# The order of the odd spreads around the sampling in a deformable convolution

## The reference

```python
om = conv3x3(x, w_off) + b_off
off_y, off_x, mask = om[:, :9], om[:, 9:18], sigmoid(om[:, 18:])
py = off_y + row + ky;  px = off_x + column + kx
sampled = bilinear(x, py, px) * mask
out = einsum('bckhw,ock->bohw', sampled, w) + b
```

## Time and profile before

| what | value |
|---|---|
| median of three runs | 2334.54 us (2331.11 to 2341.95) |
| profiled execution, span | 2334.2 us |
| PE matmul busy over the span | 1539.5 us, 66% |
| DVE busy | 1558.4 us, 67% |
| ACT busy | 1449.8 us, 62% |
| weight loader busy | 1050.0 us, 45% |
| first to last even copy of the main loop | 701.80 to 2102.34 us |

### The profile page before, as it was taken

One profiled execution on the slowest core, in us unless ns is written; L12 is line 12 of the kernel. 1 busy time (PEld: TensorE's weight loads), 2 busy tenths in 40 slices (PEclk: granted clock), 3 DMA queues, 4 the chain that ended last, 5 costly groups with the idle time before them and its releaser, 6 DMA issues. The chain is left out here.

```text
span 2334.2 us, 61913 instructions
## 1 busy us (share of the span) xinstructions
PE 1539.5 (66%) x24206; PEld 1050.0 (45%) x24207; DVE 1558.4 (67%) x1718; ACT 1449.8 (62%) x2219; POOL 606.7 (26%) x1168
## 2 busy tenths in 40 slices
PE   4755980000008888888898898898888898891620
PEld 4632330000006666666665566666665666660310
DVE  5342006656717888888888788888887888883105
ACT  2221224344218898888898898898887898890102
POOL 2000000000033444444443444444444444430000
PEclk9688995555558999999999999999999999996555
DMA  2177874667675666666666666566666656640008
GB/s 116 32 190 184 233 218 159 215 227 275 235 214 126 151 147 157 149 149 155 150 148 152 148 149 157 149 150 157 149 146 150 152 147 157 149 100 22 3 0 338
DMA packets 288861, 362.19 MB, mean 155 GB/s; under 512 B 61853, under 2 KB 260820, under 8 KB 285014
## 3 DMA queue, kind: packets, MB, share of 16 engines
q1 hardware_dynamic: 209552, 226.57, 37.6%
q0 software_dynamic: 36864, 59.94, 11.2%
q10 hardware_dynamic: 42182, 72.05, 9.0%
HBM read 253.94 MB, written 104.39 MB: 154 GB/s over the span
## 5 line engine op out<-in xcount | busy, mean ns | idle before, releaser
L758 POOL DMA_DIRECT2D rows<-scratch_parts x1152 | 583.1, 514 | 821.1 <-PE ps_even_y L790 798.8
L799 PE MATMUL ps_odd_y<-rows,sel 32*128 32x504 f32 (+2 forms) x928 | 459.8, 496 | 502.5 <-DMA rows<-scratch_parts 345.2
L939 DVE TENSOR_TENSOR G<-odd_y,ps_odd_v 128x1008 f32<-128x1008 f32 (+2 forms) x464 | 542.0, 1168 | 182.5 <-PE ps_odd_v L816 182.4
L816 PE MATMUL ps_odd_v<-tent_x,stage 32*128 32x171 f32 (+2 forms) x5568 | 591.1, 318 | 0.0
L947 DVE TENSOR_TENSOR G<-even_v,ps_even_y 128x1008 f32<-128x1008 f32 (+2 forms) x464 | 539.3, 1162 | 23.6 <-ACT even_v L895 21.7
L816 PE MATMUL ps_even_v<-tent_x,stage 32*128 32x171 f32 (+3 forms) x5568 | 541.9, 324 | 8.5 <-DMA stage<-scratch_xt 8.3
L889 ACT COPY odd_y<-ps_odd_y 128x504 f32<-128x504 f32 (+2 forms) x928 | 526.4, 567 | 21.4 <-PE ps_odd_y L799 17.1
L895 ACT COPY even_v<-ps_even_v 128x1008 f32<-128x1008 f32 (+2 forms) x464 | 450.2, 970 | 134.6 <-PE ps_odd_v L816 126.5
L834 PE MATMUL ps_r<-G,conv_w 128*32 128x224 f32 (+1 forms) x8832 | 483.3, 346 | 13.2 <-ACT res L900 13.1
L799 PEld LDWEIGHTS ps_odd_y<-rows,sel 32*128 32x128 f32 x928 | 173.0, 186 | 689.8 <-issue 350.5
L816 PEld LDWEIGHTS ps_odd_v<-tent_x,stage 32*128 32x128 f32 x5568 | 477.8, 190 | 0.0
(11 more groups left out here) (134 smaller groups left out, 913.5 us busy)
## 6 DMA issues: line engine op xcount, KB each, us to landing
place<-scratch_px SPq DMA_DIRECT2D x960, 105.0 KB, 3.4
scratch_parts<-parts ACTq DMA_DIRECT2D x18, 3136.0 KB, 16.7
rows<-scratch_parts POOLq DMA_DIRECT2D x960, 52.5 KB, 3.4
x<-scratch_xh SPq DMA_DIRECT2D x48, 406.0 KB, 5.9
place<-scratch_px SPq DMA_DIRECT2D x192, 84.0 KB, 2.7
scratch_om<-om ACTq DMA_DIRECT2D x64, 196.0 KB, 7.1
rows<-scratch_parts POOLq DMA_DIRECT2D x192, 42.0 KB, 2.6
scratch_conv<-res SPq DMA_DIRECT2D x448, 14.0 KB, 1.8
```

Source lines behind the costliest of these rows:

```text
L758: pool.dma_start(bass.AP(tensor=rows[b][:].tensor, offset=32 * g * pitch + here, ap=[[2 * pitch, Y_KINDS], [GROUP * W, 3], [1, count * W]] ...
L799: nc.tensor.matmul(ps_odd_y[:, lo:hi], sel[32 * g:32 * g + 32, :], taps(rows, 32 * g, 32, p, lo, hi), start=True, stop=True).then_inc(odd_ ...
L816: m = nc.tensor.matmul(sub(ps_v[g // 2], 0, 128, i * 512 + lo + first, dims), stage[32 * g:32 * g + 32, j * IMAGE + v * C:j * IMAGE + (v + ...
L939: nc.vector.tensor_tensor(two(G, ROW, v, slot(v)), two(odd_y[p % 3], ROW, v), two(ps_v[1], 512, v), ALU.mult).then_inc(odd_weighted, 1)
```

## The change

PE's queue in a step becomes: the first two column groups of sample(p), spread_odd(p + 1, 0), the third group, spread_even(p), spread_odd(p + 1, 1), reduce. The wait for fresh rows moves with the first odd spread. ACT copies the first odd image of step p + 1 in its step p - 1, so its queue becomes keep_even(p), keep_odd(p + 1, 1), distance(p + 2), keep_odd(p + 2, 0), result; one such copy comes before the loop. The wait of keep_odd for a free buffer is one step less strict, n - 2 for n - 1.

```diff
-                def sample(it, p):
+                def sample(it, p, to):
...
                     for j, (x0, x_lo, x_hi) in enumerate(COLUMNS):
+                        if j == 2 and to:
+                            rows_ready(*to)
+                            spread_odd(*to, 0)
...
-                        sample(it, p)
+                        sample(it, p, to)
                         spread_even(it, p)
                         if to:
-                            rows_ready(*to)
-                            spread_odd(*to, 0)
+                            spread_odd(*to, 1)
                         if at := block_of(it, p):
...
                             reduce(*at)
-                        if to:
-                            spread_odd(*to, 1)
...
                     if i == 0:
-                        wait(act, odd_weighted, n - 1)
+                        wait(act, odd_weighted, n - 2)
...
                 keep_odd(0, 0, 1)
+                keep_odd(0, 1, 0)
...
                         keep_even(it, p)
                         if to := ahead(it, p + 1, last):
-                            keep_odd(*to, 0)
+                            keep_odd(*to, 1)
                         if to := ahead(it, p + 2, last):
                             distance(*to)
-                        if to := ahead(it, p + 1, last):
-                            keep_odd(*to, 1)
+                            keep_odd(*to, 0)
```

## The result

The changed kernel takes **2452.1 us** (2441.8 to 2455.3), the kernel before 2334.0: a ratio of 1.050, 95% interval 1.048 to 1.053. It is 118 us slower, where 131 us were forecast (2465, range 2350 to 2560). The profiled execution has a span of 2449.9 us.

A forecast was written before the change was run, and what follows sets the result against it. A ring of waits through ACT's copies and the sampling, 2.94 us a step, was taken as the bound; 3.17 us steps plus longer reductions and stalls gave 95.86 for 87.72 us a pair, +130 us: 2465, range 2350 to 2560.

The forecast's parts named there:

- The bound: Kernel before: no engine full; waits through even copy, first odd copy, second odd spread and sampling set the 2.94 us step.
- the new ring: Changed step: part of sampling, first odd spread, its copy, second spread, reduction, next sampling; 3.17 us, chance 0.66.
- the one link that the trace did not have: From the first sampling matmul to the spread in the middle of the sampling: 0.68 us, bounds 0.53 to 0.83.
- The drain: Switching between 32-row and 128-row tiling empties PE: idle 0.24 us before and 0.36 us after each reduction.
- the 0.36: Idle time of the weight loader after a reduction's loads, before the next 32-row work: 0.36 us.
- The longer reductions: Reductions of 20 to 36 loads, hidden before, now count in full: 4.18 us a pair of images.
- 0.3 to 0.6 more in steps with 20 to 36 loads: Expected in the profile after: even copies 3.17 us apart in plain steps, this much further apart with longer reductions.
- The stalls: Mostly ACT's result waiting for the last store, and slower steps after: 3.5 us a pair before, 1.2 kept.
- The clock: Rival: PE slows after long waits; about 2555 us if one step in ten is hit; chance 0.15.
- The price of a slow step: A step of the changed kernel at the lower clock takes 5.16 us.
- the overlapping reduction: Rival: PE enters and leaves the reduction without idling, or the first odd copy is early; 2256 us, chance 0.12.
- the next ring: Sampling, DVE's odd product, next sampling: sets the step at 2.72 us if the main chain of waits falls below that.

The follow-up runs named there:

- The extra copies: Changed kernel plus one more ACT copy of 224 columns into a spare tile: ahead of the first odd copy 2571.1 us, ahead of the second 2442.7 us.
- two tiles: Kernel before with two tiles for the result in place of one, so ACT waits for the store before last: 2295.1 us, 0.984.
- the filled step: Changed kernel with eight more matmuls, result overwritten, in step 4 of a pair, the one step without a reduction: 2404.6 us, 1.031.
- the reversed test: Kernel before with only the second odd spread moved directly behind the first, ahead of the reduction: 3074.8 us, 1.318.

## Why the prediction was right

**The bound and the new ring** were as forecast, link by link: 0.59 for 0.68 to the middle spread, 0.55 for 0.49 + 0.04, 0.63 for 0.58 + 0.06, 0.42, and 0.89 for 0.90. The 3.09 us step is 0.08 under the 3.17, all of it the one link that the trace did not have: the spread is issued ahead of the first matmul of the third group, 1810.30 against 1810.42, not at its time. That makes 0.08 x 28 x 16 = 36 us too much in the sum. The extra copies show that the first odd copy is on the ring and the second beside it.

**The drain.** 0.24 and 0.36 us stood idle as forecast around each plain reduction, and the 0.90 came out. But the 0.36 is not a fixed price behind the last load, as the forecast took it. Behind 20 loads the loader idles 0.08 us, behind 36 loads 0.17:

```profile
1229.04 1.11 PEld L837 LDWEIGHTS ps_r<-G,conv_w 128*32 128x32 f32 x36 [0.24 <-issue]
1230.32 0.19 PEld L819 LDWEIGHTS ps_even_v<-tent_x,stage 32*128 32x128 f32 x2 [0.17 <-issue]
...
1229.04 1.35 PE L837 MATMUL ps_r<-G,conv_w 128*32 128x112 f32 x36
```

What is fixed is the distance to the matmuls. In 423 of the 443 reductions of the changed kernel that a sampling follows, the sampling's first load starts 0.07 us before the end that the profile gives for the reduction's last matmul (it models these ends): 1230.32 against 1230.39 here, 1809.71 against 1809.78 in the plain step. None starts earlier; of the 20 that start later 16 stand at the seam of two pairs. The reduction starts at the same distance from the spread ahead of it, 1811.90 against 1811.97. The rule of the Trainium skill (TensorEngine Tiling (Array Packing), Key Properties), that a change of tiling mode drains TensorE, agrees with these rows. No run was without them, so how large the part is that comes from the mode alone is not shown.

**The longer reductions**: the term of 4.18 us a pair was half wrong. A plain last quarter costs what was said: steps of 3.82 and 2.77 around it, 0.41 more than two of 3.09. But split strips cost nothing. The mis-sized step of the sum is that it added the idle 0.36 to a longer loading time. A reduction with 20 loads in the changed kernel, and the sampling behind it:

```profile
1222.85 0.81 PEld L837 LDWEIGHTS ps_r<-G,conv_w 128*32 128x32 f32 x20 [0.24 <-issue]
```

```profile
1223.74 0.41 PE L819 MATMUL ps_even_v<-tent_x,stage 32*128 32x171 f32 x2
```

It loads for 0.81 in place of 0.54 and the sampling still starts 0.89 later; steps 14 and 15 take 3.09 and 3.10. In the last quarter it is the same: the sampling comes 1.27 us behind the start of 24 loads and 1.28 behind that of 36. The columns streamed, the same number split or not, set the length, and the loader's end does not. So the sign "0.3 to 0.6 more in steps with 20 to 36 loads" came true at the last quarters only. The trace of the kernel before had it already, on PE: the matmuls of the 20 loads of the earlier trace rows lasted 0.97 us, those of 16 loads 0.96. This is 1.5 us a pair, 24 us too much.

**The stalls** were forecast to leave 1.2 of 3.5 us a pair; no wait for a store is left, since four steps now take 12.8 us for 11.8. 19 us too much. That also means that the order itself costs more than 118 us: the kernel before carries 38 us of stalls which a slower loop hides. And the 3.5 were not all stalls: two tiles took off 2.4, and in the trace of that run 0.9 a pair is left in slow steps at a lower clock.

**The clock**, a rival with 0.15, came true in part beside the forecast's case and not in place of it: some 48 us by the filled step. The sign that the forecast had set for it, a granted clock below 0.95 in the middle of the loop, was met in one stretch (0.93). The price of a slow step was right (5.16 against 4.97 to 5.06); where it would fall was not said, and that step 4 lacks its reduction stood in the text of the kernel. The holes of the earlier trace rows cut in three, 0.64, 0.24 and 0.36, leave the clock at 1.00 in plain steps, as argued.

So the sum was 36 + 24 + 19 us too high and the clock 48 too low, which leaves 31 too high; the forecast was 13 above. Of the other 18 us some 5 are three slow steps in the last pair and some 4 the slow start of the first pair; the last 9 are not assigned. The mechanism was right, but the close total is partly luck: errors of 79 and 48 us cancelled.

**The rivals**: the overlapping reduction is out, by the 0.36 of each step and by the 4.08 us step of the reversed test. That the mechanism decides at a given amount off the ring is right, but not the price at which the next ring takes over: I had it at 2.72, and with the spread behind the first third it is 2.86.

## What to carry to other kernels

An instruction that waits for another engine belongs behind the work that can fill its wait, not ahead of it: ask for each wait in an in-order queue what stands behind it, and add that to the ring. When a handover is moved earlier, check how the distance to its partner is covered; here 0.3 us, one column group, decided between 5% slower and 0.4% faster. And look at steps that lack a part of the work: they may lower the clock for the ones behind, and filling them with useless matmuls was worth 13 and 48 us in two kernels.

## What the runs showed of the hardware

- A step with PE busy for 1.77 of 3.00 us was followed, in 12 of the 15 pairs behind the first, by a fall of the granted clock to 0.50 for one to three steps (5.0 us for 3.09). With eight more matmuls in this step, 0.9 us, the clock stayed at 1.00 in all 15.
- Behind a reduction on 128 rows, the first load of the sampling on 32 rows started 0.07 us before the last matmul's end as the profile models it, whether 16, 20, 24 or 36 loads stood in the reduction; the loader's idle time was what was left, 0.36, 0.08 or 0.17 us.
- Loading weights for 20 small blocks took 0.81 us where 16 took 0.54, with the same columns to stream, and the end of the reduction did not move (0.89 us from its start).
- A spread for one strip of 32 rows in the midst of a sampling costs the sampling little: the 162-column group starts 0.71 us after the first matmul with it, 0.68 without.
